# Wider matmuls for channel means and sums, and another order of stores and loads, in a fused group-norm and gating kernel

## The reference

```python
def _L0_conv_ref(x, W1, W3):
    x = relu(x)
    avg_region = mean(x, axis=(2, 3), keepdims=True)
    peak_region = max(x, axis=(2, 3), keepdims=True)
    x = where(peak_region - avg_region < 0.5, 0.0, x)
    cmax = max(x, axis=1, keepdims=True)
    cmean = mean(x, axis=1, keepdims=True)
    bb = 1.0 - exp(-abs(cmax - cmean))
    x = bb * x
    x_max = max(x, axis=(2, 3), keepdims=True)
    pooled = mean(x, axis=(2, 3))
    control1 = sigmoid(pooled @ W1.T)[:, :, None, None]
    control3 = relu(pooled @ W3.T)
    control3 = where(control3 < 1.0, 1.2, control3)[:, :, None, None]
    thres = control1 * control3 * x_max
    return where(x < thres, 0.0, x)

x = x + _L0_conv_ref(group_norm(x, 32 groups), W1, W3)   # x: 32 x 512 x 56 x 56, float32
```

## Time and profile before

| | us |
|---|---|
| median of 3 runs | 1788.29 |
| lowest, highest | 1784.95, 1790.47 |
| profiled execution | 1780.24 |
| its span, first to last instruction | 1778.4 |

### The profile page before, as it was taken

How to read it: one execution, slowest core, us unless ns; L and a number is a source line. 1 busy time by engine, 2 the same in 40 slices (tenths; PEclk the granted TensorE clock), 3 DMA queues, 4 the chain that set the end, 5 groups by cost and what they waited for, 6 DMA issues and landing times.

```text
span 1778.4 us, 45243 instructions
## 1 busy us (share of the span) xinstructions
PE 1303.4 (73%) x19616; PEld 1080.2 (61%) x19616; DVE 1460.9 (82%) x2192; ACT 1306.6 (73%) x1921; POOL 610.6 (34%) x446
## 2 busy tenths in 40 slices
PE   4888776788876778767688777678777688777761
PEld 3766655666665666655576655566655566656660
DVE  2588887988887988888888887888887887888987
ACT  5678777777787878777767787777787767777821
POOL 0043233443233444223443233443233442233430
PEclk8898888998888898888888888898878887888885
DMA  9259989999999899998989999989999988899973
GB/s 396 87 162 301 319 315 320 281 296 297 312 330 336 277 285 306 302 329 320 287 263 296 307 330 332 283 277 296 301 330 329 279 265 269 315 329 343 296 228 145
DMA packets 93418, 518.86 MB, mean 292 GB/s; under 512 B 10272, under 2 KB 10272, under 8 KB 93216
## 3 DMA queue, kind: packets, MB, share of 16 engines
q1 hardware_dynamic: 75360, 416.38, 58.4%
q0 software_dynamic: 17856, 99.56, 28.7%
HBM read 310.38 MB, written 205.52 MB: 290 GB/s over the span
## 4 chain that ended last, share of the span: by engine, by line
PE 29%; POOL 26%; ACT 22%; DVE 15%; issue 7%; DMA 1%; SPq 0%; DVEq 0%; ACTq 0%; POOLq 0%
POOL xs L778 23%; ACT rs L476 8%; PE ps_turn L286 7%; PE ps_gate L347 7%; ACT xs L476 7%; PE ps_gate L322 6%; PE ps_gate L294 6%; DVE xs L670 6%; ACT rs L451 5%; DVE rs L670 4%; DVE max_and_mean L622 2%; POOL rstd L757 2%; DMA xs<-in_x 1%; PE ps_gate L356 1%; DVE xs L737 1%
## 5 line engine op out<-in xcount | busy, mean ns | idle before, releaser
L622 DVE TENSOR_REDUCE max_and_mean<-ps_turn 128x2 f32<-128x1024 f32 x384 | 466.0, 1220 | 201.3 <-PE ps_turn L286 200.6
L286 PE MATMUL ps_turn<-ident,xs 128*128 128x128 f32 (+1 forms) x1600 | 358.8, 310 | 177.7 <-DVE max_and_mean L622 112.3
L769 POOL DMA_DIRECT2D xs<-in_x x124 | 111.6, 968 | 940.0 <-DVE xs L670 837.0
L778 POOL TENSOR_TENSOR xs<-xs,rs 128x1568 f32<-128x1568 f32 x124 | 433.3, 3531 | 1.9 <-DVE rs L670 1.9
L286 PEld LDWEIGHTS ps_turn<-ident,xs 128*128 128x128 f32 (+1 forms) x1600 | 204.5, 153 | 311.5 <-DVE max_and_mean L622 155.2
L312 PE MATMUL ps_gate<-ident,bb 128*128 128x128 f32 (+1 forms) x1600 | 273.4, 333 | 153.2 <-ACT bb L469 144.0
L425 ACT ACTIVATE scratch<-xs 128x3136 bf16<-128x3136 f32 x128 | 360.2, 2814 | 7.8 <-DMA xs<-in_x 2.8
L312 PEld LDWEIGHTS ps_gate<-ident,bb 128*128 128x128 f32 (+1 forms) x1600 | 249.6, 239 | 173.4 <-DVE ymax_parts L639 157.7
L286 PE MATMUL ps_turn<-ident,rs 128*128 128x128 f32 (+1 forms) x1600 | 341.3, 299 | 6.0 <-issue 6.0
L639 DVE CUSTOM_DVE_ANT_0 xs<-xs,ps_gate 128x768 f32<-128x768 f32 (+1 forms) x256 | 243.3, 959 | 45.1 <-PE ps_gate L312 45.0
L451 ACT ACTIVATE xs<-xs,shift,rstd 128x3136 f32<-128x3136 f32 x64 | 191.9, 2999 | 100.0 <-POOL shift L761 93.3
(11 more groups left out here) (80 smaller groups left out, 991.9 us busy)
## 6 DMA issues: line engine op xcount, KB each, us to landing
xs<-in_x SPq DMA_DIRECT2D x260, 784.0 KB, 13.7
out<-xs SPq DMA_DIRECT2D x256, 784.0 KB, 8.2
xs<-in_x POOLq DMA_DIRECT2D x124, 784.0 KB, 11.1
rs<-in_L_conv_W SPq DMA_DIRECT2D x2, 1024.0 KB, 18.7
```

The costliest lines, as they stand in the source:

```text
L286: mm = pe.transpose(ps_turn[0:w, n % 2, b - 2 * i, P * t:P * (t + 1)], r_tile(s, t)[:, P * b:P * b + w], ident[:, :])
L622: ins = dve.tensor_reduce(max_and_mean[:, 2 * i:2 * i + 2, 0], ps_turn[:, n % 2, :, :], AX.X, ALU.max)
L778: pool.tensor_tensor(o, o, half(r_tile(s - 1, t), h), ALU.add).then_inc(added, 1)
```

## The change

- Mean rows are computed on chunks of 512 pixels instead of 128 (the last has 64): 28 matmuls a sample instead of 100. The result has 512 columns and moves in PSUM to `ps_gate[:, 0, 512:1024]`, which the gate's rows also use, so `mean_rows_of` first waits for the gates of three of the four pixel groups of the sample before.
- The means are turned by four matmuls with an operand of 7 columns instead of one with 25, and ACT copies them in another order of columns to the same place.
- The sums are computed on chunks of 448 pixels instead of 112: 28 matmuls a sample instead of 112, into `ps_gate[:, 1, 0:448]`; from the third sample on they wait for the gates of the sample before. Their wait for the copy of the logits is gone; the group statistics have it instead.
- The squares' unused output is FP8 in a tile of its own (`junk`); the control rows and the mean rows share a new tile `rows`, and copying the control rows no longer waits for the squares.
- Tiles are loaded, squared and summed in the order 0, 1, 2, 3 instead of 2, 0, 1, 3.
- SP stores the in-place tiles 0 and 1 first, each half as its accumulating transfer lands, and each load stands one or two issues behind the store that it waits for.

The diff, without comments on it:

```diff
-BF16 = mybir.dt.bfloat16
+FP8 = mybir.dt.float8e4
...
-XCHUNK = 112
+XCHUNK = 448
+MEAN_ROW = 512
-LOAD_ORDER = (2, 0, 1, 3)
+LOAD_ORDER = (0, 1, 2, 3)
...
-        scratch = sb("scratch", [P, HALF])
-        junk = scratch[:, :].bitcast(BF16)
-        control_sb = scratch[:, 0:C]
+        junk = sb("junk", [P, HW], FP8)
+        rows = sb("rows", [P, C])
+        control_sb = rows[:, :]
+        mean_rows = rows[:, 0:MEAN_ROW]
...
-        ps_mean_rows = small0[:, 0:P]
+        ps_mean_rows = ps_gate[:, 0, 512:512 + MEAN_ROW]
-        ps_rowsum = small1[:, 48:48 + XCHUNK]
+        ps_rowsum = ps_gate[:, 1, 0:XCHUNK]
...
-                store(s, 2, 0)
                 store(s, 0, 0)
                 store(s, 0, 1)
+                reload(0, 0)
+                store(s, 1, 0)
+                reload(0, 1)
+                store(s, 1, 1)
+                reload(1, 0)
+                store(s, 2, 0)
+                reload(1, 1)
                 store(s, 2, 1)
-                store(s, 1, 0)
-                store(s, 1, 1)
+                store(s, 3, 0)
                 reload(2, 0)
-                store(s, 3, 0)
-                reload(0, 0)
-                reload(0, 1)
                 reload(2, 1)
                 store(s, 3, 1)
-                reload(1, 0)
-                reload(1, 1)
                 reload(3, 0)
                 reload(3, 1)
...
             def mean_rows_of(s):
-                for t in range(T):
-                    for b in range(NBLK):
-                        w, k, j = min(P, HW - P * b), b % 4, b // 4
-                        mm = pe.matmul(ps_mean_rows[32 * k:32 * k + 32, 0:w], chan_avg[:, 31 - j:63 - j],
-                                       r_tile(s, t)[:, P * b:P * b + w], start=(t == 0 and b < 4),
+                if s > 0:
+                    pe.wait_ge(gated, T * (NG * s - 1))
+                for n in range(T * NM):
+                    t, j, k = n // NM, n % NM, n % 4
+                    w = min(MEAN_ROW, HW - MEAN_ROW * j)
+                    mm = pe.matmul(ps_mean_rows[32 * k:32 * k + 32, 0:w], chan_avg[:, 31 - j:63 - j],
+                                   r_tile(s, t)[:, MEAN_ROW * j:MEAN_ROW * j + w], start=(n < 4),
...
-                pe.matmul(ps_means, mean_rows[:, :], row_block_cols, start=True, stop=True).then_inc(means_mm, 1)
+                for i in range(MEAN_COLS):
+                    mm = pe.matmul(ps_means[:, i, :], mean_rows[:, P * i:P * (i + 1)], row_pick[:, :],
+                                   start=True, stop=True)
+                mm.then_inc(means_mm, 1)
...
             def sum_x(s, tiles):
+                if s > 1:
+                    pe.wait_ge(gated, NG * T * (s - 1))
...
-                        k = c % 4
+                        q = NX * n + c
+                        k = q % 4
...
             def group_stats(s):
                 pe.wait_ge(row_mean_ready, s + 1)
+                if s > 1:
+                    pe.wait_ge(logits_ready, s - 1)
...
-                if s > 0:
-                    pe.wait_ge(logits_ready, s)
                 if s + 1 < B:
                     sum_x(s + 1, range(0, 2))
...
-                                     accum_out=squares[:, part:part + 1])
+                                     accum_out=squares[:, part:part + 1], saturate=False)
...
-                junk_step.wait()
                 act.activation(control_sb, ps_control_rows, ACT.Identity).then_inc(control_copied, 1)
```

More of the change, by code:

```diff
@@ L54, in gated_sparsifier @@
     NX = HW // XCHUNK
+    NM = -(-HW // MEAN_ROW)
+    MEAN_COLS = MEAN_ROW // P
     GROUP_T = (0, 3, 6, 9, NT)
@@ L61, in gated_sparsifier @@
     NS = len(SUMS)
-    assert T == 4 and NBLK == 25 and LAST_W == 64 and NX * XCHUNK == HW and NX % 4 == 0 and GMAX == 832
+    assert T == 4 and NBLK == 25 and LAST_W == 64 and NX * XCHUNK == HW and NM == 7 and GMAX == 832
     x_tiles = x.rearrange("b (t p) h w -> b p t (h w)", p=P)
@@ L90, in gated_sparsifier @@
         chan_avg = sb("chan_avg", [P, 63])
-        row_block = sb("row_block", [P, 7, 4])
+        row_pick = sb("row_pick", [P, NM])
         row_part = sb("row_part", [P, 2])
-        mean_rows = sb("mean_rows", [P, P])
         ones = sb("ones", [P, 1])
@@ L113, in gated_sparsifier @@
         fkeep = sb("fkeep", [P, T])
-        max_and_mean = sb("max_and_mean", [P, NBLK, 2])
+        max_and_mean = sb("max_and_mean", [P, NM * MEAN_COLS, 2])
         diff = sb("diff", [P, NBLK])
@@ L139, in gated_sparsifier @@
         ps_control = ps_logits.rearrange("p (m o) -> p m o", o=T)
-        ps_means = small0[:, P + 4:P + 4 + NBLK]
-        ps_rowsum = small1[:, 48:48 + XCHUNK]
+        ps_means = small0[:, P + 4:P + 4 + NM * MEAN_COLS].rearrange("p (i j) -> p i j", j=NM)
+        mean_in_place = max_and_mean[:, :, :].rearrange("p (j i) c -> p i j c", i=MEAN_COLS)[:, :, :, 1]
+        ps_rowsum = ps_gate[:, 1, 0:XCHUNK]
         ps_control_rows = ps_gate[:, 0, 0:C]
@@ L188, in gated_sparsifier @@
         added_last = sem("added_last")
-        row_block_cols = row_block[:, :, :].rearrange("p j k -> p (j k)")[:, 0:NBLK]
         def x_tile(s, t):
@@ L290, in mean_rows_of @@
             def mean_rows_of(s):
-                for t in range(T):
-                    for b in range(NBLK):
-                        w, k, j = min(P, HW - P * b), b % 4, b // 4
-                        mm = pe.matmul(ps_mean_rows[32 * k:32 * k + 32, 0:w], chan_avg[:, 31 - j:63 - j],
-                                       r_tile(s, t)[:, P * b:P * b + w], start=(t == 0 and b < 4),
-                                       stop=(t == T - 1 and b >= NBLK - 4), skip_group_check=True,
-                                       tile_position=(0, 32 * k))
+                if s > 0:
[5 more added lines that the diff above has]
+                                   r_tile(s, t)[:, MEAN_ROW * j:MEAN_ROW * j + w], start=(n < 4),
+                                   stop=(n >= T * NM - 4), skip_group_check=True, tile_position=(0, 32 * k))
                 mm.then_inc(mean_rows_mm, 1)
@@ L320, in sum_x @@
                     for c in range(NX):
-                        k = c % 4
+                        q = NX * n + c
+                        k = q % 4
                         mm = pe.matmul(ps_rowsum[32 * k:32 * k + 32, :], sel[:, t, :],
                                        x_tile(s, t)[:, XCHUNK * c:XCHUNK * (c + 1)],
-                                       start=(n == 0 and c < 4), stop=(n == T - 1 and c >= NX - 4),
+                                       start=(q < 4), stop=(q >= NX * T - 4),
                                        skip_group_check=True, tile_position=(0, 32 * k))
@@ L437, in row_means @@
                 steps.step(act.activation(junk[:, 0:XCHUNK], ps_rowsum, ACT.Identity,
-                                          scale=1.0 / (PER_GROUP * HW), accum_out=row_sum[:, :]))
+                                          scale=1.0 / (PER_GROUP * HW), accum_out=row_sum[:, :], saturate=False))
                 steps.wait()
@@ L459, in copy_means @@
                 act.wait_ge(means_mm, s + 1)
-                act.activation(max_and_mean[:, :, 1], ps_means, ACT.Identity, scale=-1.0).then_inc(means_ready, 1)
+                act.activation(mean_in_place, ps_means, ACT.Identity, scale=-1.0).then_inc(means_ready, 1)
             def gate_values(s, g):
@@ L550, in _ @@
                               AX.XY, ALU.add)
-            dve.tensor_copy(row_block[:, :, :], ident[:, :].rearrange("p (k r) -> p r k", k=4)[:, 0:7, :])
+            dve.tensor_reduce(row_pick[:, :], ident[:, :].rearrange("p (k r) -> p r k", k=4)[:, 0:NM, :], AX.X,
+                              ALU.add)
             dve.tensor_reduce(row_group[:, :], ident[:, :].rearrange("p (a g) -> p g a", g=8), AX.X, ALU.add)
```

## The result

The changed kernel takes 1803.9 us (median of 14 runs), the kernel before 1787.7 us in as many runs beside it: ratio 1.0087, interval [1.0055, 1.0119]. Forecast were 1738 us and "faster". The profiled execution of the changed kernel took 1796.8 us with a span of 1795.0, 16.6 us over the span before.

A forecast was written before the change was run, and what follows sets the result against it. It took PE's instruction-fetch gaps to close the loop in 17 of 29 samples. Samples of 51.45 us (1492 against 1542.4) save 50 from 1780.2, so 1730, plus 8 for the median: 1738 us, range 1718 to 1762.

The forecast's parts named there:

- The gaps: PE standing before ACT's copy of group statistics, taken as missing fetched instructions; 3.08 us in each of 17 samples, 52 us.
- DVE's keeps close the loop: After the change DVE's keeps end last before POOL's affine in every sample, 51.45 us each; further PE gain is worth nothing.
- the products' row: Profile row of PE's 512-column control products, 8 passes in 0.97 us; its 0.121 us a pass priced the mean rows.
- the dense piece: PE's mean rows and sums before the change, 424 pairs of load and matmul in 11.5 us, needing 3.3 instruction packets.
- rival 3: ACT's FP8 squares are 0.19 us dearer each, 0.4 us past the keeps, 12 us in all: 1750 us; chance 0.07.
- The branch: PE's path from logits to affine, beside DVE's keeps; forecast to end at 965.3 us, the keeps at 965.46.
- Rival 2: PE's wide passes overlap less: 1.7 us a sample, 0.7 past the keeps, 20 us in all, 1758 us; chance 0.09.
- rival 4: PE's gaps are not instruction fetching and stay: 1788 to 1802 us, say 1795; chance 0.05.
- part 5: SyncE's new order of stores and reloads and the tile order: earlier loads give nothing, 0 us, unless the queues run empty.
- rival 1: SyncE's order starves transfers: a reload waiting for its store leaves 1.3 us empty; four such +30 us, 1818; chance 0.09.

The follow-up runs named there:

- experiment 1: The changed kernel with SyncE's order and the tile order of the kernel before, so the wide matmuls, FP8 squares and moved waits stay: 1722.9 us, ratio 0.9644.
- experiment 5: The kernel of experiment 1 with the sums over x on 112 columns again, mean rows still on 512: 1742.1 us, ratio 0.9764.
- experiment 3: The changed kernel with the in-place stores still early but their reloads moved behind tile 2's first store and further back: 1723.6 us, ratio 0.9644.
- experiment 4: The changed kernel with tile 2's first store ahead of all again and two stores between an in-place store and its reload: 1723.1 us, ratio 0.9641.
- experiment 6: The changed kernel with POOL's four transfers a sample as plain copies of x instead of accumulating ones: 1722.8 us, ratio 0.9661.
- experiment 7: The changed kernel with each reload one store further back on SyncE: 1721.6 us, ratio 0.9652.
- experiment 2: The kernel before with the new order on SyncE and the new tile order, matmuls as they were: 1828.8 us, ratio 1.0225.

## Why the prediction was wrong, point by point

**Right: what bounded the kernel before and what the wide matmuls do.** The gaps went (packets 154 to 78), DVE's keeps close the loop in all later samples of experiment 1, and the loop is 51.20 us; 1738 was forecast for this, 1723 measured. Of these 15 us, 7 are 0.23 us in 29 samples against the 51.45 I had taken from one sample, and 7 are the median, which lay 8 us over the profiled execution before and 1.4 in experiment 1.

**Off, without effect.** Mean rows: 6.05 us taken, 5.5 measured (the products' row was the wrong neighbour, columns alone gave 5.5). Sums: two halves of 3.2 us, where 5.9 was taken for both; 14 matmuls in four column groups are three and a half rounds, and 3.2 us is what four full ones would take (8 x 448 columns x 0.875 ns = 3.14). The means' eight passes took 1.06 us, not 0.79. The part of a sample outside the dense piece is 42 us (53.2 - 11.5), not 44, which changes no count of packets. PE's timeline in experiment 1:

```profile
873.24 3.18 PE L331 MATMUL ps_gate<-xs,sel 128*32 128x448 f32 x28
876.35 1.06 PE L306 MATMUL ps_gate<-row_pick,rows 128*128 128x7 f32 x8
877.33 3.20 PE L331 MATMUL ps_gate<-xs,sel 128*32 128x448 f32 x28
```

ACT's squares with FP8 output take 2812 ns, against 2814 with BF16, so rival 3 fell; the copy of 512 columns takes 581 ns (599 taken), row means 544 (0.55 expected). The branch ended 0.3 us before the keeps; 0.2 was forecast. Rival 2 fell with the mean rows, and rival 4 with the packets and experiment 5.

**The step that failed: part 5, "0, unless the queues run empty", and the price of rival 1.** Three sentences of it were wrong.

- "A store lands 3.3 us after issue at best, while it uses the engines for 2.0", so 1.3 us for each exposed wait. What counts is not the best landing but the one in the queue at that place: 12.7, 9.8, 9.4 and 8.5 us in the chain above. The row I used gave min, median and max (3.3, 8.2, 16.7); I took the minimum. With the median, four hops of a store and its reload's issue are some 35 us, and it was the sum along SyncE's program that had to be made.
- "Each reload stands two transfers behind its store, so one other is in flight." In flight is not the question, and the DMA engines were not short of work: in the chain above, from 867 to 930 us, the DMA share is 0.93 to 1.02. The stores behind the reload are held, whatever is in flight, and the store of tile 3 went out 8 us later than in experiment 3, which has the same early stores.
- "Nobody waits for a load now except at the start, so an earlier load gives nothing: 0". It was a later load that had to be priced. The last load before had little slack: in the kernel before it landed 4 to 6 us after the next sample's logits and is wanted by the last square and the last sums 9 to 10 us after them. That is some 4 us of room. I summed engine time (49 of 51.45 us) and never laid the last load's landing against its use, though the landings were in the trace.

The size of a miss was not seen either. In nine samples of the changed kernel the last load goes out 0.6 to 1.5 us after the next sample's first accumulating issue, and these nine need 8.8 to 11.3 us to land; the other twenty (from the third sample on) go out earlier, or 0.3 us after it in one, and need 4.1 to 6.5 us. So 1 us too late becomes 7 to 10 us at the affine. That makes nine samples cost 71 us while the others cost next to nothing. In experiments 3, 4, 6 and 7 the last load is ahead of that issue in every sample, by 0.3 to 3.8, 2.6 to 4.6, 4.9 to 8.6 and 5.0 to 6.7 us, and each gives back everything at once: 72 to 77 us of span, not a part.

**Direction.** The kernel got slower, where faster had 0.85. Rival 1 had 0.09, with 1818 us for four exposed waits. It named the right place (SyncE's order) and the right sign (PE and ACT wait for loads of x), but not the mechanism: the DMA engines did not stand empty. The two data queues' shares are 62.3% and 28.3% in the changed kernel and 60.1% and 29.7% in experiment 1. That its 1818 us lie within 1% of the measured time is luck.

## What to carry to other kernels

When a queue's program gets a wait, sum the landings along the program as they are under load, from the median of the landings at that place and not the least, and lay the last transfer's landing against its first use; shares of busy time do not show it. Here, where stores land in some 10 us, a reload with one other store between it and its own was too close, and with two it cost nothing. And test the parts of a change apart: here one part was worth -3.6% and the other +2.2% alone and some +4.6% on top of the first, and with one further reordering on ACT (-6.3%) the order on SyncE decided whether that showed at all.

## What the runs showed of the hardware

Transfers of 784 KB that accumulate and plain ones on the other queue slow each other: accumulating ones land 11.0 us after issue on the median with the old order and 13.3 (up to 18.1) with stores beside them; a store issued while they land needs 7.9 to 12.8 us, where the least is 3.3. That is not theirs alone: with the old order the last stores, issued close behind others and beside loads, need up to 16.7 us. POOL's fourth accumulating issue waits until the first has landed: it starts 0.3 us after that landing in all 31 samples, before and changed ("issue" before L778, up to 6.7 us in the changed kernel, 4.4 before), so what slows the first transfer also delays POOL. With plain transfers (experiment 6) the fourth starts 0.6 to 1.4 us before the first has landed.

PE can run out of instructions in a dense piece of short ones: 424 pairs in 11.5 us gave gaps in 17 of 29 samples, 280 pairs in experiment 5 some, 112 none. The Trainium skill (Runtime: NRT & Kernel Launch, Instruction fetch mechanics) has fetching hidden behind issue. The runs do not agree with that: all 68 gaps over 0.7 us in the kernel before and in experiments 2 and 5 end 1.2 to 1.6 us after an instruction packet.

Four column groups with 512 columns ran mean rows in 5.5 us; the columns alone, at the 0.22 ns of the narrow passes, are 5.5 us, so the overlap was complete as far as that figure goes. The Trainium skill (TensorE: Matmul & The Clock Gate, Measured speedup vs the span model) has 2.38 times for three column groups, four fifths of ideal; the trace here is better than that.
